# Causal attention: the exponentials of one head taken bank by bank, in three operations in place of one

## The chip, the core and the metric

One core of a Trainium2 chip runs the whole program: TensorE (PE), VectorE (DVE), ScalarE (ACT), GpSimd (POOL) and the DMA queues each work through an instruction list of their own in order and meet only at semaphores. The metric is the device time of one execution in microseconds (us).

## The reference, cut to what matters

A decoder block: causal self-attention over 4 sequences of 512 rows (16 heads of 32 columns, rotary positions), residual and layer norm, cross attention on a top-54 selection, a second norm, and a feed-forward stage with eight weighted experts. The change lies in the first part only:

```python
scale = jnp.float32(1.0 / np.sqrt(HEAD_DIM))
scores = jnp.einsum('bhqd,bhkd->bhqk', qf, kf) * scale
causal = jnp.triu(jnp.ones((S, S), dtype=bool), k=1)
scores = jnp.where(causal, -jnp.inf, scores)
weights = jax.nn.softmax(scores, axis=-1)
out = jnp.einsum('bhqk,bhkd->bhqd', weights, v)
```

## The kernel before

Stage A is the self-attention. A loop over the four sequences runs, on every engine, an order of steps written out by hand (`A_PE`, `A_ACT`, `A_DVE`, `A_POOL`), in which the heads of one sequence are interleaved with the projections of the next. A step has a name and a number: `bk.9` is step `bk` of head 9. For each head:

- `bq` (PE): scores with queries on the partitions, into banks 0 to 2. `max` (DVE, L1539) takes the negated row maxima from them, four reductions a head. Every fourth head, `mT` (PE, L987) turns four heads' maxima, and DVE (L1549) writes them as extra rows of the query operand `qcT`, so that the next scores come out with the maximum already subtracted.
- `bk` (PE, L999 and L1001): scores with keys on the partitions, into banks 3 to 5 (`st_ps`), of which there is one set. Only the causal part is computed: key block t needs 512, 384, 256 or 128 columns for t = 0 to 3. Each block is one product (L999) and one small product that adds the mask on its diagonal square (L1001). `OFF` places block 0 in bank 3, blocks 1 and 3 in bank 4, block 2 in half of bank 5: 1280 columns in a row.
- `exp` (ACT, L1253): the exponential of all 1280 columns, from the three banks into `pf[:, i % 2]`, of which there are two.
- `hi` (ACT) rounds `pf` to float16 in `phi`, and `lo` (DVE L1553 or POOL L777) writes the remainder to `plo`; 12 of the 16 heads do this (`HALVED`). Heads 3, 7, 11 and 15 don't.
- `pv` (PE): the product with the values, from `phi` and `plo` (L1018 to L1020, 30 short products) or, for those four heads, from the float32 `pf` itself (L1015, 20 products). ACT then copies the result to `osb`.

`bk` of the next head waits until `exp` of this one is through (`exp_done`), since both use the same three banks. `exp` waits for `bk` of its head (`st_ready`), and for `lo` or `pv` of two heads earlier, which free the buffer `pf`. In the program order of the last steps of a sequence, PE runs `bk.9 ... pv.7 bk.10 pv.8 ... bk.11 mT.3 pv.9 ... bk.12 pv.10 ... bk.13 pv.11 bk.14 pv.12 bk.15 pv.13`, and ACT runs `exp.9 pv.7 hi.9 exp.10 pv.8 hi.10 exp.11 pv.9 exp.12 pv.10 hi.12 exp.13 pv.11 hi.13 exp.14 pv.12`. The steps `q0`, `k0`, `q1`, `k1` (PE L962) turn the rows of Q and K for the scores; ACT copies K to `kcT` and DVE copies Q to `qcT`. The last sequence has no next one, so its engines run only the steps of its own heads, with the first weight of the cross attention (`wqw`) put in behind `pv.12` on ACT.

Stage B is the cross attention and stage C the feed-forward part; the change does not touch them. They begin when the last `pv` of stage A has been copied.

Of the kernel before, what the change touches and what calls it, by code (L numbers as in the profile page):

```python
# [16 lines left out]
ACT = mybir.ActivationFunctionType  # L17
# [7 lines left out]
H, HD, NOPE = 16, 32, 8  # L25
# [22 lines left out]
TRI = sum((i + 1) * P for i in range(TT))  # L48

OFF = {4: 0, 3: 512, 1: 896, 2: 1024}  # L50

# [214 lines left out]
def decoder(nc, a):  # L268
    ctx = ExitStack()

    def sem(name):
        return ctx.enter_context(nc.semaphore(name))
# [4 lines left out]
    with ctx:  # L277
# [139 lines left out]
        nm_ready = sem("nm_ready")  # L417
        st_ready = sem("st_ready")
        exp_done = sem("exp_done")
        p_hi = sem("p_hi")  # L420
        p_lo_pool = sem("p_lo_pool")
        p_lo_dve = sem("p_lo_dve")
# [302 lines left out]
        @block.gpsimd  # L725
        def _(pool):

            for s in [max_done, st_ready, exp_done, p_lo_pool, p_lo_dve, roped, cat_lo, nm_ready, v_moved[0], v_moved[1], comb_done, res_read,
                      att_ready, x2_kept] + \
                    [d[k] for d in (a_ready, a_drained) for k in A_PER] + [d[k] for d in (b_ready, b_drained) for k in B_BANK] + \  # L730
                    [b_low[k] for k in COPIED]:
                pool.sem_inc(s, FREE)
# [170 lines left out]
        def _(pe):  # L903
# [11 lines left out]
            def heads(seq, b, nxt, earlier, first=0, end=None):  # L915

                for n, (k, i) in enumerate(seq[:end]):
# [10 lines left out]
                    if k == "xT":  # L928

                        if i == 0:  # L930
                            pe.wait_ge(x_loaded, own * 16 + 16)
                        for t in range(TT):
                            mm = nc.tensor.transpose(bank[:, t * P:(t + 1) * P], x_in[:, t, i * P:(i + 1) * P], identf[:, :])
                        mm.then_inc(done, 1)
                    elif k == "c":

                        pe.wait_ge(w_lo, 2)
                        pe.wait_ge(a_drained["xT"], a_upto(own, ("xT", DT - 1)))
                        three(bank, lambda x, j: wkvd[:, x, j, :], lambda y, j: xT[:, y, j, :], DT, done)
                    elif k == "row":  # L940
                        ts = slice(i // 2 * P, (i // 2 + 1) * P)
                        if i == 0:
                            pe.wait_ge(w_lo, 1)
                            pe.wait_ge(a_drained["xT"], a_upto(own, ("xT", DT - 1)))
                        if i % 2 == 0:
                            three(bank, lambda x, j: xT[:, x, j, ts], lambda y, j: wq[:, y, j, :], DT, done)
                        else:
                            if i == 1:
                                pe.wait_ge(w_lo, 4)
                                pe.wait_ge(a_drained["c"], a_upto(own, ("c", 0)))  # L950
                            three(bank, lambda x, j: cT[:, x, ts], lambda y, j: wku[:, y, :], 1, done)
                    elif k == "v":
                        if i == 0:
                            pe.wait_ge(a_drained["c"], a_upto(own, ("c", 0)))
                        three(bank, lambda x, j: cT[:, x, i * P:(i + 1) * P], lambda y, j: wvu[:, y, :], 1, done)
                    elif k in ("q0", "k0", "q1", "k1"):
                        row = 2 * i + (k[0] == "k")
                        pe.wait_ge(cat_lo, own * (2 * TT) + (row + 1 + FREE))
                        out = bank.bitcast(F16)
                        for j in range(8):  # L960
                            src = cat[:, row, (k[1] == "1") * 8 + j].rearrange("p a n -> p (a n)")
                            mm = nc.tensor.transpose(out[0:K3, j * P:(j + 1) * P], src, ident16[:, :])  # L962
                        mm.then_inc(done, 1)
                    elif k in ("bq", "bqn"):

                        free = i - 1 if b is None and 0 < i < G else i
                        pe.wait_ge(max_done, (own * H + free) * 4 + FREE)
                        score = max_bank(b, i)
                        if k == "bqn" and i == 0:
                            for name in ("q0", "k0"):  # L970
                                pe.wait_ge(a_drained[name], a_upto(own, (name, TT - 1)))
                        if k == "bq" and i == 8:
                            for name in ("q1", "k1"):
                                pe.wait_ge(a_drained[name], a_upto(own, (name, TT - 1)))
                        for t in range(TT):
                            w = (t + 1) * P
                            o = OFF[t + 1]
                            nc.tensor.matmul(score[:, o:o + w], qcT[0:K3, i, t * P:(t + 1) * P], kcT[0:K3, i, 0:w],  # L978
                                             start=True, stop=False)
                            mm = nc.tensor.matmul(score[:, o + w - P:o + w], identb[:, :], mask_qk[:, :],  # L980
                                                  start=False, stop=True)
                        mm.then_inc(max_ready, 1)
                    elif k in ("mT", "mTn"):
                        pe.wait_ge(nm_ready, own * (H // G) + (i + 1 + FREE))
                        out = bank.bitcast(F16)
                        for t in range(TT):
                            mm = nc.tensor.transpose(out[:, t * P:(t + 1) * P], nm16[:, t, :], ident16[:, :])  # L987
                        mm.then_inc(done, 1)
                    elif k == "bk":

                        if i == 0:
                            pe.wait_ge(own_rows, 2)
                        if i % G == 0:
                            pe.wait_ge(a_drained["mT"], a_upto(own, ("mT", i // G)))
                        pe.wait_ge(exp_done, own * H + (i + FREE))
                        for t in range(TT):
                            w = S - t * P
                            o = OFF[TT - t]
                            nc.tensor.matmul(st_ps[:, o:o + w], kcT[0:K3 + G, i, t * P:(t + 1) * P],  # L999
                                             qcT[0:K3 + G, i, t * P:S], start=True, stop=False)  # L1000
                            mm = nc.tensor.matmul(st_ps[:, o:o + P], identb[:, :], mask_kq[:, :], start=False, stop=True)  # L1001
                        mm.then_inc(st_ready, 1)
                    elif k == "pv":

                        wait_low(pe, own, i)
                        if i not in HALVED:
                            pe.wait_ge(exp_done, own * H + (i + 1 + FREE))
                        if i % 8 == 0:
                            pe.wait_ge(v_moved[i // 8], own * 16 + (16 + FREE))
                        for q in range(TT):  # L1010
                            out = bank[:, q * (HD + 1):(q + 1) * (HD + 1)]
                            for t in range(q + 1):
                                o = OFF[TT - t] + (q - t) * P
                                if i not in HALVED:
                                    mm = nc.tensor.matmul(out, pf[:, i % 2, o:o + P], vcat[:, place(i), t, :], start=t == 0, stop=t == q)  # L1015
                                    continue
                                high, low = vcat_halved[:, place(i), t, 0:HD + 1], vcat_halved[:, place(i), t, HD + 2:2 * HD + 2]
                                nc.tensor.matmul(out, phi[:, i % 2, o:o + P], high, start=t == 0, stop=False)  # L1018
                                nc.tensor.matmul(out[:, 0:HD], phi[:, i % 2, o:o + P], low, start=False, stop=False)
                                mm = nc.tensor.matmul(out, plo[:, i % 2, o:o + P], high, start=False, stop=t == q)  # L1020
                        mm.then_inc(done, 1)
# [180 lines left out]
        def _(act):  # L1202
# [5 lines left out]
            def heads(seq, b, nxt):  # L1208
                for k, i in seq:
# [34 lines left out]
                        scaled(dst, rows[:, i % 4].unsqueeze(2).to_broadcast([P, H, 2, HD]), 1.0).then_inc(cat_hi, 1)  # L1244
                    elif k == "exp":
                        g = own * H + i
                        act.wait_ge(st_ready, g + (1 + FREE))
                        of, before = (own, i - 2) if i >= 2 else (own - 1, i + H - 2)
                        if before in HALVED:
                            wait_low(act, of, before)  # L1250
                        else:
                            act.wait_ge(a_ready["pv"], a_upto(of, ("pv", before)))
                        nc.scalar.activation(pf[:, i % 2, :], st_ps[:, 0:TRI], ACT.Exp,  # L1253
                                             scale=1.0 / (SQ * SQ * math.sqrt(HD))).then_inc(exp_done, 1)
                    elif k == "hi":
                        g = own * H + i
                        act.wait_ge(exp_done, g + (1 + FREE))
# [688 lines left out]
```

## Time and profile before

| | us |
|---|---|
| median of 3 runs | 1645.51 (1641.74 to 1646.3) |
| the profiled execution | 1652.47 |
| its span from first to last instruction | 1650.6 |
| stage A's four passes, in that span | about 98 to 457 |

The profile is of one execution. Its rows give start times in us from the start of the span, and durations. A matmul's row lasts longer than it keeps the array from the next one, since matmuls are pipelined: the distance from start to start is what a stream costs. The same holds for two ACT operations in a row. PEclk is TensorE's granted clock as a share of 2.4 GHz.

### The profile page before, as it was taken

What the parts mean: (1) busy time and instruction counts of PE and PEld (TensorE: products, weight loads), DVE (VectorE), ACT (ScalarE), POOL (GpSimd) and SP (SyncE); (2) the same over time, 40 slices, a digit from 0 to 9 for tenths busy, and PEclk for the clock granted to TensorE, in tenths of its full rate; (3) what the DMA queues carried; (4) which work ended last, traced back from release to release, by engine and by line L of the source; (5) the groups of instructions that cost most, each with busy time, mean ns of one, the idle gap of its engine ahead of it and who ended that gap; (6) DMA issues with size and microseconds to landing.
All of it is one profiled execution on the core that took longest, in us unless ns stands there. A gap on an engine that the chain in (4) does not pass through costs nothing.

```text
span 1650.6 us, 27696 instructions
## 1 busy us (share of the span) xinstructions
PE 1468.6 (89%) x10404; PEld 900.5 (55%) x10404; DVE 1193.6 (72%) x2027; ACT 900.6 (55%) x1448; POOL 777.5 (47%) x693
## 2 busy tenths in 40 slices
PE   6788887987778898577899999999999999999984
PEld 2356656565644444233555665566556655665554
DVE  2767696978359999976766676767677667767757
ACT  3447576765545544455565556555655565456542
POOL 2726171631123214678554465446644664456422
PEclk8878899997589999878999999999999999999998
DMA  9500010003010200120000100010011001000002
GB/s 287 207 26 2 28 53 29 27 15 116 27 51 27 77 29 23 51 77 14 26 27 26 39 27 26 28 38 26 27 35 30 26 26 39 26 26 27 14 1 102
DMA packets 68148, 74.68 MB, mean 45 GB/s; under 512 B 9008, under 2 KB 46512, under 8 KB 66992
## 3 DMA queue, kind: packets, MB, share of 16 engines
q1 hardware_dynamic: 67440, 68.68, 12.8%
q10 hardware_dynamic: 576, 4.19, 0.7%
q8 instruction: 88, 1.44, 0.4%
q14 instruction: 44, 0.36, 0.1%
HBM read 49.66 MB, written 10.49 MB: 36 GB/s over the span
## 4 chain that ended last, share of the span: by engine, by line
PE 66%; DVE 15%; issue 9%; ACT 4%; POOL 4%; SPq 1%; DMA 0%; DVEq 0%; ACTq 0%; POOLq 0%
PE banks L1161 48%; PE banks L908 7%; DVE nmf L1539 3%; PE banks L1015 2%; PE banks L978 2%; PE banks L962 2%; PE banks L999 2%; ACT pf L1253 1%; DVE top L1663 1%; DVE wk L1659 1%; DVE cat L1522 1%; DVE attf L1670 1%; POOL mid L885 1%; PE banks L980 1%; PE banks L1108 1%
## 5 line engine op out<-in xcount | busy, mean ns | idle before, releaser
L1161 PE MATMUL banks<-xc,w 128*128 128x512 f16 x2688 | 587.8, 381 | 16.6 <-ACT banks L1204 16.6
L1161 PEld LDWEIGHTS banks<-xc,w 128*128 128x128 f16 x2688 | 263.3, 98 | 335.3 <-ACT banks L1204 22.7
L1161 PE MATMUL banks<-wd,mid 128*128 128x256 f16 x2688 | 298.2, 273 | 5.2 <-ACT banks L1204 3.1
L1161 PEld LDWEIGHTS banks<-wd,mid 128*128 128x128 f16 x2688 | 263.5, 98 | 40.9 <-ACT banks L1204 3.4
L885 POOL TENSOR_TENSOR mid<-m,mid 128x512 f16<-128x512 f32 x64 | 74.5, 1164 | 316.2 <-ACT mid L1204 316.1
L1204 ACT ACTIVATE banks<-banks 128x512 f32<-128x512 f32 x192 | 108.4, 578 | 185.6 <-PE banks L1161 185.5
L885 POOL TENSOR_TENSOR mid<-msum,mid 128x512 f16<-128x512 f32 x128 | 185.7, 1470 | 1.3 <-ACT mid L1204 1.3
L1485 DVE SCALAR_TENSOR_TENSOR w<-stage,w 128x512 f16<-128x512 f32 (+1 forms) x56 | 61.4, 1137 | 106.1 <-ACT w L1204 106.1
L1204 ACT ACTIVATE mid<-msum 128x512 f16<-128x512 f32 x128 | 81.1, 634 | 85.5 <-DVE msum L1846 29.2
L1539 DVE TENSOR_REDUCE nmf<-banks 128x1 f32<-128x512 f32 (+3 forms) x256 | 107.3, 481 | 19.7 <-PE banks L980 19.2
L777 POOL TENSOR_TENSOR plo<-pf,phi 128x1280 f16<-128x1280 f32 x24 | 63.5, 2650 | 122.1 <-ACT phi L1204 122.0
L1253 ACT ACTIVATE pf<-banks 128x1280 f32<-128x1280 f32 x64 | 79.2, 1237 | 45.2 <-PE banks L1001 25.5
L767 POOL TENSOR_TENSOR turn_a<-rows,cossin 128x384 f32<-128x384 f32 x32 | 36.6, 1145 | 123.8 <-ACT rows L1204 122.8
L1204 ACT ACTIVATE xc<-banks 128x512 f32<-128x512 f32 (+1 forms) x112 | 62.8, 599 | 49.9 <-PE banks L1108 28.9
L885 POOL TENSOR_TENSOR mid<-xc,mid 128x512 f16<-128x512 f32 x32 | 52.5, 1641 | 69.3 <-ACT mid L1204 69.3
L999 PE MATMUL banks<-qcT,kcT 100*128 100x512 f16 (+3 forms) x256 | 70.9, 353 | 12.5 <-ACT pf L1253 11.8
L978 PE MATMUL banks<-kcT,qcT 96*128 96x128 f16 (+3 forms) x256 | 67.2, 339 | 14.8 <-DVE nmf L1539 13.6
L1485 DVE SCALAR_TENSOR_TENSOR wd<-stage,wd 128x512 f16<-128x512 f32 (+1 forms) x32 | 29.6, 966 | 65.7 <-ACT wd L1204 65.7
L1808 DVE TENSOR_TENSOR xc<-banks,xc 128x512 f32<-128x512 f32 x96 | 63.1, 681 | 17.3 <-ACT banks L1204 17.2
L1808 DVE TENSOR_TENSOR s<-banks,s 128x512 f32<-128x512 f32 x96 | 64.1, 683 | 14.2 <-PE banks L1161 14.2
L1204 ACT ACTIVATE s<-banks 128x512 f32<-128x512 f32 x96 | 56.3, 602 | 27.0 <-PE banks L1161 26.9
L1204 ACT ACTIVATE phi<-pf 128x1280 f16<-128x1280 f32 x48 | 60.9, 1270 | 0.9 <-PE banks L1020 0.9
(252 smaller groups left out, 2981.6 us busy)
## 6 DMA issues: line engine op xcount, KB each, us to landing
stage<-w_fold SPq DMA_DIRECT2D x24, 256.0 KB, 3.0
stage<-in_Wg SPq DMA_DIRECT2D x24, 256.0 KB, 3.1
stage<-in_Wu SPq DMA_DIRECT2D x24, 256.0 KB, 3.1
stage<-in_Wd SPq DMA_DIRECT2D x24, 256.0 KB, 2.8
vcat<-vnext SPq DMA_DIRECT2D x8, 528.0 KB, 3.4
x_in<-in_x SPq DMA_DIRECT2D x4, 1024.0 KB, 6.6
x_res<-in_x SPq DMA_DIRECT2D x4, 1024.0 KB, 6.0
c_raw<-in_ctx SPq DMA_DIRECT2D x4, 1024.0 KB, 5.5
```

The source lines that it names most:

```text
L767: nc.gpsimd.tensor_tensor(dst[:, :, :, :], pair, cs, ALU.mult).then_inc(roped, 1)
L777: nc.gpsimd.tensor_tensor(plo[:, i % 2, :], pf[:, i % 2, :], phi[:, i % 2, :], ALU.subtract).then_inc(p_lo_pool, 1)
L885: nc.gpsimd.tensor_tensor(mid16[:, v % 3, 1, blk], mid_value(name), mid16[:, v % 3, 0, blk], ALU.subtract)\
L908: mm = nc.tensor.matmul(out, l(x, i), r(y, i), start=(i == 0 and j == 0), stop=(i == n - 1 and j == 2))
L978: nc.tensor.matmul(score[:, o:o + w], qcT[0:K3, i, t * P:(t + 1) * P], kcT[0:K3, i, 0:w], start=True, stop=False)
L999: nc.tensor.matmul(st_ps[:, o:o + w], kcT[0:K3 + G, i, t * P:(t + 1) * P], qcT[0:K3 + G, i, t * P:S], start=True, stop=False)
L1161: mm = nc.tensor.matmul(out, l(x, i), r(y, i), start=start and i == 0 and j == 0, stop=stop and i == k - 1 and j == 2, skip_group_check=True)
L1204: return nc.scalar.activation(out, in_, ACT.Copy, scale=scale)
L1253: nc.scalar.activation(pf[:, i % 2, :], st_ps[:, 0:TRI], ACT.Exp, scale=1.0 / (SQ * SQ * math.sqrt(HD))).then_inc(exp_done, 1)
L1485: return stt(out=out, in0=src, scalar=scale, in1=hi, op0=ALU.mult, op1=ALU.subtract)
L1539: nc.vector.tensor_reduce(nmf[:, t, i % G:i % G + 1], max_bank(b, i)[:, o:o + w], AX, ALU.max, negate=True)\
L1808: tt_(saved, banks[:, k, :], saved, ALU.add).then_inc(c_sum, 1)
```

## The change

`exp` of a head becomes three ACT operations, of 512, 512 and 256 columns, one for each bank. The first two signal a new semaphore `exp_part`, the last signals `exp_done` as before. PE issues the blocks of `bk` in the order 0, 1, 3, 2, so that bank 4 is complete before bank 5 is begun; after block 0 and after block 3 it signals another new semaphore, `st_part`, and after block 2 `st_ready` as before. Before blocks 0, 1 and 2 PE waits only for the previous head's exponential of that one bank, where one wait for all three stood ahead of block 0. Each of the three ACT operations waits for the scores of its own bank.

```diff
+ST_ORDER = (0, 1, 3, 2)
+ST_FIRST = (0, 1, 2)
+ST_LAST = (0, 3, 2)
+ST_COLS = ((0, 512), (512, 1024), (1024, 1280))
...
@@ PE, bk
-                        pe.wait_ge(exp_done, own * H + (i + FREE))
-                        for t in range(TT):
+                        for t in ST_ORDER:
+                            if t in ST_FIRST:
+                                part = ST_FIRST.index(t)
+                                if part < 2:
+                                    pe.wait_ge(exp_part, (own * H + i) * 2 + (part - 1 + FREE))
+                                else:
+                                    pe.wait_ge(exp_done, own * H + (i + FREE))
...
                             mm = nc.tensor.matmul(st_ps[:, o:o + P], identb[:, :], mask_kq[:, :], start=False, stop=True)
+                            if t in ST_LAST[:2]:
+                                mm.then_inc(st_part, 1)
                         mm.then_inc(st_ready, 1)
@@ ACT, exp
-                        act.wait_ge(st_ready, g + (1 + FREE))
...
-                        nc.scalar.activation(pf[:, i % 2, :], st_ps[:, 0:TRI], ACT.Exp,
-                                             scale=1.0 / (SQ * SQ * math.sqrt(HD))).then_inc(exp_done, 1)
+                        for part, (c0, c1) in enumerate(ST_COLS):
+                            if part < 2:
+                                act.wait_ge(st_part, g * 2 + (part + 1))
+                            else:
+                                act.wait_ge(st_ready, g + (1 + FREE))
+                            nc.scalar.activation(pf[:, i % 2, c0:c1], st_ps[:, c0:c1], ACT.Exp,
+                                                 scale=1.0 / (SQ * SQ * math.sqrt(HD))).then_inc(exp_part if part < 2 else exp_done, 1)
```

## Rows read from the trace of the kernel before

**Rows 1.** Stretches: PE, PEld, DVE, ACT, POOL busy us, then PEclk, DMA, GB/s.

```profile
282.00:374.00 92.00, 80.44 (x975) 59.19 (x976) 73.61 (x133) 65.87 (x86) 43.51 (x38) 0.96 0.08 25
405.00:457.00 52.00, 39.53 (x448) 32.70 (x447) 24.71 (x35) 25.83 (x35) 10.35 (x12) 0.60 0.06 21
```

**Rows 2.** Waits in stage A, 98 to 457: total us, times, longest.

```profile
ACT pf L1253 <- PE banks L1001: 25.5, 27, 4.4
ACT pf L1253 <- PE banks L1015: 19.8, 8, 4.7
PE banks L999 <- ACT pf L1253: 11.8, 12, 1.4
```

**Rows 3.** Chain that ended last, shares by line, 98 to 457.

```profile
by line: issue 12.7%; DVE nmf L1539 10.8%; PE banks L1015 9.3%; PE banks L999 8.0%; PE banks L978 7.1%; PE banks L908 6.7%; PE banks L962 6.2%; ACT pf L1253 4.8%; PE banks L1001 3.1%; PE banks L980 2.8%; ACT kcT L1204 2.6%; DVE cat L1522 2.
```

**Rows 4.** The same chain in time, last sequence: start us, us, what.

```profile
416.29 1.25 ACT pf L1253
...
421.63 1.25 ACT pf L1253
...
428.07 1.24 DVE qcT L1549
...
434.04 4.23 PE banks L1015 x20
...
438.35 1.25 ACT pf L1253
...
442.49 0.27 ACT osb L1204
```

**Rows 5.** The same chain in the third pass, `exp.13` and `bk.14`.

```profile
358.05 1.25 ACT pf L1253
...
359.34 0.39 PE banks L999
```

**Rows 6.** ACT in order of time, third pass: start us, us, operation.

```profile
306.13 0.59 ACT L1204 ACTIVATE rows<-banks 128x512 f32<-128x512 f32 x1
306.61 1.06 ACT L1204 ACTIVATE cat<-rows 128x1024 f16<-128x1024 f32 x1
...
343.63 1.24 ACT L1253 ACTIVATE pf<-banks 128x1280 f32<-128x1280 f32 x1 [1.16 <-PE banks L1015]
344.76 0.28 ACT L1204 ACTIVATE osb<-banks 128x132 f32<-128x132 f32 x1
344.92 1.02 ACT L1204 ACTIVATE kcT<-banks 96x1024 f16<-96x1024 f16 x1
...
348.27 1.28 ACT L1204 ACTIVATE phi<-pf 128x1280 f16<-128x1280 f32 x1
349.43 1.03 ACT L1204 ACTIVATE kcT<-banks 96x1024 f16<-96x1024 f16 x1
```

**Rows 7.** PE in order of time, last sequence: `bk.9`, then `bk.10` to `bk.11`.

```profile
417.58 0.39 PE L999 MATMUL banks<-qcT,kcT 100*128 100x512 f16 x1 [0.58 <-ACT pf L1253]
...
418.38 0.22 PE L978 MATMUL banks<-kcT,qcT 96*128 96x128 f16 x1
...
422.92 0.61 PE L999 MATMUL banks<-qcT,kcT 100*128 100x512 f16 x1 [1.39 <-ACT pf L1253]
...
423.43 0.53 PE L999 MATMUL banks<-qcT,kcT 100*128 100x384 f16 x1
...
423.86 0.42 PE L999 MATMUL banks<-qcT,kcT 100*128 100x256 f16 x1
...
424.18 0.31 PE L999 MATMUL banks<-qcT,kcT 100*128 100x128 f16 x1
...
424.39 0.23 PE L1018 MATMUL banks<-vcat,phi 128*128 128x33 f16 x1
...
425.26 0.19 PE L1020 MATMUL banks<-vcat,plo 128*128 128x33 f16 x1
425.93 0.61 PE L999 MATMUL banks<-qcT,kcT 100*128 100x512 f16 x1 [0.48 <-ACT pf L1253]
```

**Rows 8.** PE in the third pass: end of `bk.2`, then `k1.2`.

```profile
295.50 0.22 PE L1001 MATMUL banks<-mask_kq,identb 128*128 128x128 bf16 x1
295.79 0.31 PE L962 MATMUL banks<-ident,cat 128*96 128x128 f16 x2
```

**Rows 9.** DVE at the same time.

```profile
294.97 0.69 DVE L1529 COPY qcT<-banks 96x1024 f16<-96x1024 f16 x1 [0.39 <-PE banks L962]
```

## What it does to the time: the prediction, before the changed kernel was run

> **What bounds the kernel now.** I read the busy times of the stretches first, then the waits of stage A, then the chain that ended last, and only then single instructions. Stage A takes some 359 us of the span. In one inner pass no engine is full: PE 80 us of 92, DVE 74, ACT 66 [rows 1]. The reader is to see that the pass hangs on the order in which the engines hand work to each other. In the last sequence's second half (405 to 457), where only its own heads are left, PE is busy 40 us of 52, DVE and ACT half the time, and TensorE's granted clock is 0.60 on average, so much of it runs at the lower level of 1.2 GHz [rows 1].
>
> The waits say how much the change can touch. ACT stands 25.5 us in all for `bk` before an exponential, and another 19.8 us for the float32 `pv` that frees its buffer; PE stands 11.8 us for exponentials before `bk` [rows 2]. Those are upper limits. The chain says how little of it counts: over stage A, L1253 holds 4.8% of the chain, some 17 us, which is about 14 of the 64 exponentials; the rest of the time DVE's reductions, the projections and the transposes are last [rows 3]. So the change is worth something only at those places, and I price them one by one.
>
> **The price of three ACT operations.** Spacing from start to start is what counts on a busy ACT: 1.13 us for the 1280 columns (343.63 to 344.76), 0.16 for 132 columns (344.76 to 344.92), 0.48 for 512 columns out of PSUM (306.13 to 306.61) [rows 6]. A line through the first two is 0.05 us fixed and 0.845 ns a column, and gives 0.48 for 512, as measured. Two more operations therefore cost 2 x 0.05 = 0.10 us a head: 0.48 + 0.48 + 0.27 = 1.23 in place of 1.13. No row shows two exponentials of one head in a row, so the bounds are 0 below and, above, no overlap at all: the durations 0.59 + 0.59 + 0.38 = 1.56 (the last on a line between 0.28 and 1.24) less 1.24, so 0.32 us. I take 0.10, since operations that wait for semaphores already satisfied stand in these same rows at the close spacing. From the start of the first part to the end of the third it is then 0.48 + 0.48 + 0.38 = 1.34 us, and the first part is done after 0.59, the second after 1.07.
>
> The Trainium skill speaks against the split here: ScalarE: Activation LUTs, section What ACT_TABLE_LOAD costs, gives an ACTIVATE with immediate scale a fixed 186 ns, of which about 93 overlap when two follow each other. By that page the split costs about 0.19 us a head (an estimate), and the sum below would be 0.5 us smaller. The trace, with 0.05 us fixed, makes it cheaper.
>
> **The price of two more waits on PE.** Where the semaphore is long satisfied I take nothing. After `bk.9`, `bq.15` has a wait in front of it and starts 418.38, 0.80 us after `bk.9` started, with no gap [rows 7]. The nearest thing that speaks against it is `k1.2`: it starts 0.29 us after the last mask product of `bk.2`, which occupies only 0.06, so 0.23 us of gap [rows 8]. But DVE's copy, which frees its bank, ends 295.66, just before [rows 9]: that gap is a wait satisfied late. Bounds: 0 and 0.23 us a wait. The new increments and the order 0, 1, 3, 2 move no column and cost nothing; they are covered by PE's own pipeline, and without that cover would cost at most what a wait does. Queued behind PE's new waits are the rest of `bk` and the next `pv` or `bq`; behind ACT's, the `osb` copy and `hi`. None of them would run earlier today, because the single wait they replace ended later or as late. The wait for the freed `pf` now stands ahead of the scores' wait, which changes nothing, since both must pass.
>
> **What a link gains at the lower clock.** `bk.10` starts 422.92, 1.29 us after `exp.9` (421.63) [rows 4, 7]. Its blocks take 0.51, 0.43, 0.32 and 0.21 us with their masks, 1.47 in all, and `pv.8` follows with 30 products up to 425.29, so 0.90 [rows 7]. I count from the start of `exp.9`. Before: `bk.10` from 1.29 to 2.76, `bk.11` from 4.30 (425.93) [rows 7]. After: block 0 can start at 0.59 + 0.05 = 0.64 (0.05 being the step from 1.24 to 1.29) and ends 1.15; blocks 1 and 3 end 1.58 and 1.79 (the second part was done at 1.07); block 2 ends 2.11 (the third was done at 1.34). `pv.8` ends at 3.01. ACT meanwhile runs `exp.9`, `osb` and `hi`: 1.23 + 0.16 + 1.16 (348.27 to 349.43 [rows 6]) = 2.55, when `exp.10` starts; its first part is done at 3.14, so `bk.11` starts at 3.19 and ends block by block at 3.70, 4.13, 4.34 and 4.66 (the third part is done at 3.89). Before, it ended at 4.30 + 1.47 = 5.77. So `bk.11`, and behind it `mT.3` and DVE's copy at 428.07 [rows 4], come 1.1 us earlier.
>
> The next links, in the same way. `bk.12` waits for DVE's copy; `exp.12` starts when bank 3 is ready instead of all three, and `bk.13` no longer waits behind the whole of it. DVE's copy, now at 5.34, is followed by `bk.12` at 6.63 (1.24 for the copy [rows 4] and the step of 0.05), blocks done 7.14, 7.57, 7.78 and 8.10; `exp.12`'s parts are done about 7.97, 8.63 and 8.90; `pv.10` ends 9.00, and `bk.13` runs right behind it, so the float32 `pv.11` starts at about 10.65 instead of 12.41 (434.04 [rows 4]): 0.65 us more. Then `exp.13`, which waits for `pv.11`, and `bk.14` are one more link; there ACT's order sets the end: `exp.13`, `osb`, `hi.13`, `exp.14`, and the copy of `pv.12` stands 2.55 + 1.23 = 3.78 us after `exp.13`, where it stands 4.14 now (438.35 to 442.49 [rows 4]): 0.35. One link earlier, `bk.9` stood 0.58 us idle for `exp.8` (416.29) at the upper clock [rows 4, 7]; `pv.6` lies between, and with it the idle goes: 0.55.
>
> Last sequence: 1.1 + 0.65 + 0.35 + 0.55 = 2.65 us. What is late next there is ACT and DVE with `wqw`, which follow `pv.12` on ACT directly and so move with it, then the last `pv`, then stage B, whose first work waits for that.
>
> **The three passes before.** Around 343 to 349 ACT runs without a pause from `exp.9` to the K copy at 349.43 [rows 6], for which PE waits; all scores are there, so two split exponentials make it 2 x 0.10 = 0.20 us later. Then `exp.13` to `bk.14` (358.05 to 359.34 [rows 5]) gains: `bk` takes 0.80 us at the upper clock [rows 7], so it ended at 1.29 + 0.80 = 2.09; after, block 2 ends at 1.34 + 0.05 + 0.17 = 1.56. That is 0.53. Net 0.33 a pass; POOL's remainder for head 13, whose `hi` comes 0.3 us later behind two split exponentials, holds it to about 0.25 at `pv.13`. Elsewhere in the pass DVE is last and exponentials have slack. Three passes: 0.75 us.
>
> **Sum.** 1652.47 - 2.65 - 0.75 = 1649.1 for the profiled execution, 3.4 us or 0.2% less. It stands 7 us above the median of the runs, so on the median's scale 1645.5 - 3.4 = 1642.1. A measurement of this kernel can tell about 0.3%, 4.9 us, from no change, so the forecast is no change that can be told. With the bounds of the ACT price (0 to 0.32 a part-split head) the sum is about 1641 to 1644.
>
> **Rivals.**
> - *The clock comes along.* In the last sequence the clock is full at `bk.9` and half from `bk.10` on, after PE stood 1.39 us [rows 7]. The change shortens that stop to about 0.64. If the upper level holds to `pv.11`, that one costs some 2.2 us less than its 4.23 [rows 4] and three groups `bk` on the chain 0.67 each (1.47 against 0.80): 4.2 us more, 1638. Against it: stops of 0.5 us remain at every head. The same thing with the other sign: the clock stays low where it is now high (`bk.9`, `bq.15`, `pv.7`), about 3.8 us, which gives 1646. The Trainium skill, TensorE: Matmul & The Clock Gate, section A second HAM failure mode, describes frequent short idles between groups of matmuls making the clock swing; that would be this second sign. No row here shows which.
> - *The gain does not arrive.* ACT's price is at its upper end and the gains of the links go to it: three passes at 2 x 0.32 - 0.53 = +0.1 each, the last sequence with four links at 0.22 less each, 1.8. Then 1644.
> - *Slower: each new wait holds back PE's next weight load.* If a wait costs the 0.23 us of [rows 8] even when satisfied, then with L999 on 8.0% of 359 us of chain [rows 3], about 29 us, at 0.56 to 1.04 us of it a group, some 40 groups are on the path: 40 x 2 x 0.23 = 18 us, 1660. It decides from (4.9 + 3.4) / 80 = 0.10 us a wait. Against it stands the late release that explains that gap.
> - *It does not do what it says:* if ACT still begins after all scores (its own order holds it), only the price is left, 1646. That lies inside the case before.
>
> **Chances.** Forecast 0.48 (its own range 1640 to 1645), clock with gain 0.24, gain lost or clock lost 0.15, slower by waits 0.13. Faster by over 0.3%: the clock case and 0.07 of the forecast's edge, 0.31. Within: 0.56. Slower: 0.13. The range takes in the clock case and the start of the slow one and leaves out about 0.2: 1636 to 1650.
>
> **What would show it.** Right: three ACT rows a head of about 0.59, 0.59 and 0.38 us, close together where scores are ready; PE's waits for ACT before `bk` shrinking by half; the copy of `pv.12` about 2.6 us nearer to `exp.8`; ACT's idle before exponentials [rows 2] smaller, most of it worth nothing. Wrong: gaps of 0.2 us inside `bk` groups whose exponential is long done; part spacing over 0.6 us; another granted clock after 415; or DVE's reductions moving, which the sum holds still.

## The result, and the profile after

The changed kernel took 0.9946 of the time of the one before, 95% interval 0.9926 to 0.9966, from 20 runs of each (medians 1643.81 and 1651.4 us). One run of the changed kernel took 2205.66 us at a granted clock of 0.64, where the others have 0.94, and is left out of the ratio. The ratio is worth 8.9 us, between 5.6 and 12.2. The forecast was 3.4 us less, too little to be told from no change. The profiled execution of the changed kernel has a span of 1642.1 us, where the one before had 1650.6.

Single executions of one kernel scatter by some 12 to 20 us: in the fourteen profiled ones the first transposes of the inner passes begin anywhere between 88.2 and 98.6 us, in code that no kernel here changes. So spans say little, and the traces are compared by stretches that begin and end at the same instruction. Landmarks are the starts of the float32 products `pv.3`, `pv.7`, `pv.11` and `pv.15` of the last sequence.

Line numbers have moved: `exp` is L1272 (before: L1253), `bk` L1012 (L999), its mask L1014 (L1001), float32 `pv` L1030 (L1015), ACT's copies L1219 (L1204), POOL's `lo` L785 (L777), DVE's normalisation L1601 (L1582).

First, stage A's waits in the changed kernel (columns as in rows 2):

```profile
ACT pf L1272 <- PE banks L1030: 16.0, 8, 3.1
PE banks L1012 <- ACT pf L1272: 5.5, 9, 1.1
ACT pf L1272 <- PE banks L1014: 4.3, 5, 1.5
```

ACT's wait for scores ahead of an exponential fell from 25.5 to 4.3 us, PE's wait for exponentials from 11.8 to 5.5 [rows 2]. Now the windows (columns as in rows 1): one inner pass, and the last 52 us before stage B starts, which in time lie 10.5 us earlier than the window of [rows 1]:

```profile
279.20:371.20 92.00, 80.78 (x966) 58.85 (x967) 73.14 (x132) 67.73 (x119) 43.38 (x38) 0.96 0.07 24
394.46:446.46 52.00, 42.18 (x502) 33.90 (x501) 31.81 (x56) 32.81 (x65) 10.70 (x12) 0.72 0.12 44
```

The pass is as before. The end of the last sequence is not: more work fits into 52 us, and TensorE's granted clock is 0.72 on average in place of 0.60 [rows 1].

Where that comes from is seen on PE, in order of time, from `pv.7` to `pv.11`:

```profile
413.64 2.37 PE L1030 MATMUL banks<-vcat,pf 128*128 128x33 f32 x20
416.70 0.39 PE L1012 MATMUL banks<-qcT,kcT 100*128 100x512 f16 x1 [0.69 <-ACT pf L1272]
...
419.28 0.61 PE L1012 MATMUL banks<-qcT,kcT 100*128 100x512 f16 x1
...
422.39 0.39 PE L1012 MATMUL banks<-qcT,kcT 100*128 100x512 f16 x1
422.67 0.33 PE L1012 MATMUL banks<-qcT,kcT 100*128 100x384 f16 x1
422.90 0.22 PE L1012 MATMUL banks<-qcT,kcT 100*128 100x128 f16 x1
423.01 0.27 PE L1012 MATMUL banks<-qcT,kcT 100*128 100x256 f16 x1
...
424.91 0.38 PE L1012 MATMUL banks<-qcT,kcT 100*128 100x512 f16 x1
...
425.71 2.37 PE L1030 MATMUL banks<-vcat,pf 128*128 128x33 f32 x20
```

`bk.10` starts after a pause of 0.69 us, where it was 1.39, and its first product takes 0.39 us, where it took 0.61 [rows 7]. `bk.11` falls to the lower level (0.61), `bk.12` and `bk.13` are at the upper one again, and so is `pv.11`: 2.37 us, 4.42 before. The granted clock of the same two stretches, `pv.7` to `pv.11` and `pv.11` itself, first in the kernel before, then after:

```profile
419.17:433.83 14.66, 11.83 (x148) 9.38 (x147) 5.72 (x10) 9.22 (x11) 5.23 (x2) 0.61 0.01 2
433.83:438.25 4.42, 4.42 (x22) 4.29 (x20) 1.33 (x1) 0.00 (x0) 0.00 (x0) 0.50 0.00 0
```

```profile
413.64:425.70 12.06, 9.90 (x148) 7.75 (x147) 6.65 (x9) 8.57 (x20) 5.20 (x2) 0.86 0.01 2
425.70:428.08 2.38, 2.38 (x22) 2.26 (x20) 1.31 (x1) 1.04 (x1) 0.00 (x0) 1.00 0.01 3
```

0.50 and 1.00 are the levels of 1.2 and 2.4 GHz. Next, ACT:

```profile
341.49 1.36 ACT L1272 ACTIVATE pf<-banks 128x512 f32<-128x512 f32 x3 [1.19 <-PE banks L1030]
342.73 0.30 ACT L1219 ACTIVATE osb<-banks 128x132 f32<-128x132 f32 x1
...
421.46 1.36 ACT L1272 ACTIVATE pf<-banks 128x512 f32<-128x512 f32 x3
...
424.05 1.36 ACT L1272 ACTIVATE pf<-banks 128x512 f32<-128x512 f32 x3 [1.05 <-POOL plo L785]
```

Three parts are shown as one row (x3) of 1.36 us where the single operation took 1.24; from the start of `exp.9` to the start of the next copy are 1.24 us where it was 1.13 [rows 6]. The last two rows are `exp.11` and `exp.12` of the last sequence. They no longer wait for scores: POOL's `lo.9` and `lo.10`, back to back from 418.81 to 424.01, hold their buffers:

```profile
418.81 5.20 POOL L785 TENSOR_TENSOR plo<-pf,phi 128x1280 f16<-128x1280 f32 x2 [12.28 <-ACT phi L1219]
```

The last rows were no part of the prediction. The first fence is the kernel before in another execution, ACT, DVE and POOL around `exp.5` of the last sequence, the second the changed kernel. The DVE row marked x4 is four operations, and the row below it is the fourth of them alone:

```profile
399.24 1.28 ACT L1253 ACT_TABLE_LOAD   x1
401.93 1.24 ACT L1253 ACTIVATE pf<-banks 128x1280 f32<-128x1280 f32 x1 [1.41 <-PE banks L1001]
...
403.24 4.21 DVE L1582 TENSOR_SCALAR resid<-resid,mv,rstd 128x512 f32<-128x512 f32 x4
404.62 2.84 DVE L1582 TENSOR_SCALAR resid<-resid,mv,rstd 128x512 f32<-128x512 f32 x1
...
404.55 2.62 POOL L777 TENSOR_TENSOR plo<-pf,phi 128x1280 f16<-128x1280 f32 x1 [19.80 <-ACT phi L1204]
```

```profile
399.88 1.28 ACT L1272 ACT_TABLE_LOAD   x1 [1.79 <-PE banks L1014]
401.18 1.36 ACT L1272 ACTIVATE pf<-banks 128x512 f32<-128x512 f32 x3
...
402.11 1.92 DVE L1601 TENSOR_SCALAR resid<-resid,mv,rstd 128x512 f32<-128x512 f32 x4
403.49 0.54 DVE L1601 TENSOR_SCALAR resid<-resid,mv,rstd 128x512 f32<-128x512 f32 x1
...
403.92 2.62 POOL L785 TENSOR_TENSOR plo<-pf,phi 128x1280 f16<-128x1280 f32 x1 [18.04 <-ACT phi L1219]
```

Before, the table load for the exponential runs ahead of the wait for scores, inside the pause; after, it follows that wait. And the four normalisations of DVE take 4.21 us before and 1.92 after. The difference lies in the fourth one: in the kernel before POOL's `lo.5` begins 0.07 us ahead of it and it lasts 2.84 us, after the change `lo.5` begins 0.43 us behind it and it lasts 0.54.

### The profile page after: what moved, and what is told of

Same layout as the page of the kernel before. It is cut to its first block, busy times and chain, and to the rows that moved or that the text cites. A ratio compares the mean times of both kernels' runs of the same rounds, so it can differ in the third digit from the quotient of the medians.

```text
span 1642.1 us, 27967 instructions
## 1 busy us (share of the span) xinstructions
PE 1466.6 (89%) x10404; PEld 897.5 (55%) x10404; DVE 1193.5 (73%) x2027; ACT 907.7 (55%) x1576; POOL 777.2 (47%) x693
## 4 chain that ended last, share of the span: by engine, by line
PE 64%; DVE 14%; issue 12%; POOL 6%; ACT 3%; SPq 1%; DMA 0%; DVEq 0%; POOLq 0%; ACTq 0%
PE banks L1176 48%; PE banks L916 7%; DVE nmf L1558 2%; PE banks L986 2%; PE banks L970 1%; PE banks L1030 1%; POOL plo L785 1%; DVE top L1682 1%; DVE wk L1678 1%; PE banks L1012 1%; DVE cat L1541 1%; DVE attf L1689 1%; PE banks L1123 1%; POOL mid L893 1%; POOL xsum L820 1%
## 5 line engine op out<-in xcount | busy, mean ns | idle before, releaser
L1219 ACT ACTIVATE banks<-banks 128x512 f32<-128x512 f32 x192 | 108.4, 578 | 185.6 <-PE banks L1176 185.5
L1504 DVE SCALAR_TENSOR_TENSOR w<-stage,w 128x512 f16<-128x512 f32 (+1 forms) x56 | 61.5, 1137 | 106.0 <-ACT w L1219 106.0
L1219 ACT ACTIVATE mid<-msum 128x512 f16<-128x512 f32 x128 | 81.1, 634 | 85.5 <-DVE msum L1865 29.2
L785 POOL TENSOR_TENSOR plo<-pf,phi 128x1280 f16<-128x1280 f32 x24 | 63.1, 2635 | 114.0 <-ACT phi L1219 114.0
L1272 ACT ACTIVATE pf<-banks 128x512 f32<-128x512 f32 (+1 forms) x192 | 87.5, 533 | 22.3 <-PE banks L1030 16.0
L1219 ACT ACTIVATE xc<-banks 128x512 f32<-128x512 f32 (+1 forms) x112 | 62.8, 598 | 49.9 <-PE banks L1123 28.9
L986 PE MATMUL banks<-kcT,qcT 96*128 96x128 f16 (+3 forms) x256 | 66.8, 338 | 12.2 <-DVE nmf L1558 11.0
L1012 PE MATMUL banks<-qcT,kcT 100*128 100x512 f16 (+3 forms) x256 | 66.5, 333 | 6.2 <-ACT pf L1272 5.5
L1219 ACT ACTIVATE s<-banks 128x512 f32<-128x512 f32 x96 | 56.2, 603 | 26.9 <-PE banks L1176 26.9
L1219 ACT ACTIVATE phi<-pf 128x1280 f16<-128x1280 f32 x48 | 61.5, 1281 | 2.1 <-PE banks L1035 2.1
```

The lines of the kernel that those rows point to most:

```text
L785: nc.gpsimd.tensor_tensor(plo[:, i % 2, :], pf[:, i % 2, :], phi[:, i % 2, :], ALU.subtract).then_inc(p_lo_pool, 1)
L1219: return nc.scalar.activation(out, in_, ACT.Copy, scale=scale)
L1272: nc.scalar.activation(pf[:, i % 2, c0:c1], st_ps[:, c0:c1], ACT.Exp, scale=1.0 / (SQ * SQ * math.sqrt(HD))).then_inc(exp_part if part < 2 ...
L1504: return stt(out=out, in0=src, scalar=scale, in1=hi, op0=ALU.mult, op1=ALU.subtract)
```

## The experiments

Theory A: the gain lies in the last sequence, where scores and exponentials alternate. Theory B: it is what the forecast's sum says, 2.65 us there and 0.25 us in each pass. Theory C, formed after the first four runs: most of the gain in the last sequence is TensorE's upper clock. (In the expectation for last_only, C still means that the gain is an accident of the clock and of the time at which DVE and POOL meet.) Ratios are to the kernel before, on the same chip, with 95% intervals. The table has the stretches of each trace, in us from start to start ("to B": from `pv.15` to ACT's first operation of stage B that writes `cxT`).

| | ratio | `pv.3` to `pv.7` | to `pv.11` | to `pv.15` | to B |
|---|---|---|---|---|---|
| before | 1 | 22.92 | 14.66 | 15.98 | 6.92 |
| before, again | | 24.52 | 14.11 | 15.97 | 6.92 |
| after | 0.9946 (0.9926 to 0.9966) | 18.69 | 12.06 | 13.57 | 6.92 |
| after, again | | 18.69 | 12.06 | 13.56 | 6.91 |
| last_only | 0.9944 (0.9920 to 0.9969) | 18.69 | 12.05 | 13.56 | 6.92 |
| inner_only | 1.0013 (0.9986 to 1.0039) | 21.77 | 14.62 | 15.99 | 6.92 |
| act_half | 0.9980 (0.9957 to 1.0002) | 20.37 | 13.64 | 15.76 | 6.92 |
| pe_half | 0.9948 (0.9920 to 0.9977) | 20.33 | 12.49 | 13.56 | 6.92 |
| price | 1.0001 (0.9971 to 1.0030) | 22.01 | 15.10 | 16.22 | 6.91 |
| fill_before | 0.9981 (0.9955 to 1.0007) | 24.53 | 12.49 | 15.00 | 6.86 |
| fill_after | 0.9959 (0.9933 to 0.9985) | 19.95 | 12.39 | 15.31 | 6.86 |
| fill_scores | 0.9983 (0.9954 to 1.0013) | 24.51 | 12.57 | 13.38 | 6.91 |
| tail_heads | 0.9934 (0.9911 to 0.9958) | 19.95 | 12.84 | 13.56 | 6.92 |
| tail_fill | 0.9929 (0.9903 to 0.9955) | 19.95 | 12.61 | 13.46 | 4.57 |

`pv.3` itself is at the upper clock in before (2.37 us), partly so in after, after again and last_only (2.8), and at the lower one (4.42) in all others. With the same exponentials that makes 1.3 to 1.6 us in the first of these stretches (18.69 against 19.95, 22.92 against 24.52). The columns are compared with this in mind.

**Where: last_only and inner_only.** The head sets say in which heads the split and the waits per bank are used.

```diff
+SPLIT_INNER = ()               # last_only; inner_only: tuple(range(H))
+SPLIT_LAST = tuple(range(H))   # last_only; inner_only: ()
...
+                        if i not in cut:
+                            act.wait_ge(st_ready, g + (1 + FREE))
+                            nc.scalar.activation(pf[:, i % 2, :], st_ps[:, 0:TRI], ACT.Exp, scale=scale).then_inc(exp_done, 1)
```

> The three-part exponential and the bank-wise waits in the last sequence only; the three passes before it as in the kernel before. Theory A (the gain comes from the last sequence, where bk and exp alternate with little else between, and the passes give about nothing): the last sequence's end comes some 8 us earlier counted from the last pass's start, as in the changed kernel, and the time is 0.994 to 0.997 of before. Theory B (the forecast's ledger, 2.65 us there and 0.25 us in each pass): 0.998. Theory C (the profile's gain in the last sequence is an accident of the clock and of the time at which DVE and POOL meet): 0.999 to 1.000.

> The reverse: the change in the three passes only, the last sequence as in the kernel before. Theory A: each pass as long as before within 0.3 us, time 0.999 to 1.001. Theory B: 0.75 us less, 0.9995. If the gain were spread over all 64 heads, three quarters of it would stand here: 0.996.

last_only gives the whole gain and inner_only none that can be told. Theory A holds, and B's 0.998 lies outside the interval of last_only. The two kernels before and after also differ in the order of ACT's two waits, and both of these have the new order in every head.

**Which wait: act_half and pe_half.** In act_half ACT takes each bank on its scores, while PE waits for the whole exponential; in pe_half PE takes the banks back one by one, while ACT waits for all scores.

```diff
@@ act_half, PE
+                        pe.wait_ge(exp_done, own * H + (i + FREE))
                         for t in ST_ORDER:
@@ pe_half, ACT
+                        act.wait_ge(st_ready, g + (1 + FREE))
                         for part, (c0, c1) in enumerate(ST_COLS):
```

> Half of the change: ACT runs the three parts, each on its bank's scores, but PE waits for the whole exponential of the previous head before bk, as before. By the prediction's rows exp.10 then starts 2.55 us after exp.9 instead of 3.01, but bk.11 only at 3.94 (before 4.30, with both halves 3.19). If both halves matter alike, half the gain is left; by these rows a third: the last sequence 1 to 3 us shorter, time 0.998 to 0.999.

> The other half: PE takes each bank as soon as its exponential is through, but ACT waits for all scores of a head before its three parts. By the prediction's rows ACT's own order (exp, osb, hi, 2.55 us) is later than the scores (2.35), so nothing is lost by that wait: the last sequence nearly as short as in the changed kernel, 6 to 8 us less than before, time 0.995 to 0.997. If starting ACT early is what pays, it is close to before.

PE's side carries most of the gain: from `pv.3` to stage B, pe_half takes 53.3 us, act_half 56.7, inner_only 59.3. In pe_half `pv.11` took 2.37 us, in act_half 4.42. That suggested theory C. Over all fourteen traces `pv.11` is at the upper clock in the seven in which PE takes the banks early, and otherwise only in fill_before and fill_scores below; it is at the lower one in before (both executions), inner_only, act_half and price.

**The clock alone: fill_before, fill_scores and fill_after.** The kernel before gets spare products on PE in the last sequence, into a bank that no one reads any more; all its waits and operations stay, and one wait is added, for the row maxima that free this bank.

```diff
+            def keep_busy(n, first=False):
+                if first:
+                    pe.wait_ge(max_done, B * H * 4 + FREE)
+                for _ in range(n):
+                    nc.tensor.matmul(banks[:, 0, 0:P], ident16[:, :], ident16[:, :], start=True, stop=True)
...
@@ ahead of bk's wait
+                        if isinstance(own, int) and own == B - 1 and i >= 10:
+                            keep_busy(6, i == 10)
@@ ahead of pv (fill_before and fill_after only)
+                        if isinstance(own, int) and own == B - 1 and i >= 14:
+                            keep_busy(24 if i == 14 else 4)
```

> The kernel before, its exponentials whole, with spare 128-column products on TensorE in the last sequence: 6 ahead of the scores of each of heads 10 to 15, 24 ahead of pv.14 and 4 ahead of pv.15 (their result is read by nothing). Theory C (what the three parts give beyond their links in the last sequence is TensorE's upper clock, which the shorter pauses between score groups keep up): with the pauses filled and nothing else changed, pv.11 and pv.15 take about 2.1 us each where they take 4.0 to 4.2, so some 2 us each and the score groups beside them a little; 3 to 5 us faster than before, ratio 0.997 to 0.998. Rival (the links do it all, the clock only goes along): pv.11 may come out at 2.1 us and the end hardly moves, 0.9995 to 1.001; and the fill itself costs where it stands on the path, up to 0.35 us for each of the 6 heads, 2 us, 1.001.

> The same spare products in the changed kernel. There pv.11 is at the upper clock already, and pv.15 alone still took 4.08 us. Theory C: pv.15 falls to about 2.1 us, so some 2 us faster than the changed kernel, 0.993 against before. Rival (links): no different from the changed kernel, 0.9945, or 1 to 2 us slower by the fill, 0.9955.

> The kernel before with only the 6 spare products ahead of the scores of heads 10 to 15 in the last sequence (none ahead of pv.14 and pv.15, where in the run with the long fill they ended 1.2 us after pv.14 could have started). Theory C (the upper clock gives most of it): from pv.7 to pv.15 some 26.3 us, where the kernel before took 30.64, the changed kernel 25.63 and the run with the long fill 27.49; pv.11 at 2.4 us from first start to last end; 4 us faster than before, 0.997 to 0.998. Rival (the waits for banks themselves give it): pv.7 to pv.15 no less than 29 us, 0.999 to 1.000.

fill_scores, PE, POOL and ACT in order of time and then the windows from `pv.7` to `pv.11` and of `pv.11` (in this kernel the fill is L918, `bk` L1007, `exp` L1261, float32 `pv` L1023; the POOL row is `lo.9` and `lo.10`, the ACT row `exp.12`):

```profile
413.27 0.50 PE L918 MATMUL banks<-ident 128*128 128x128 f16 x6
414.82 0.39 PE L1007 MATMUL banks<-qcT,kcT 100*128 100x512 f16 x1 [1.05 <-ACT pf L1261]
...
416.17 5.20 POOL L777 TENSOR_TENSOR plo<-pf,phi 128x1280 f16<-128x1280 f32 x2 [16.94 <-ACT phi L1212]
...
421.54 1.24 ACT L1261 ACTIVATE pf<-banks 128x1280 f32<-128x1280 f32 x1 [1.15 <-PE banks L1009]
...
423.63 2.37 PE L1023 MATMUL banks<-vcat,pf 128*128 128x33 f32 x20
```

```profile
411.06:423.62 12.56, 11.19 (x172) 9.26 (x171) 5.84 (x9) 8.51 (x11) 5.20 (x2) 0.86 0.01 3
423.62:426.00 2.38, 2.38 (x26) 2.38 (x24) 1.49 (x1) 0.49 (x1) 0.00 (x0) 1.00 0.00 0
```

With whole exponentials and nothing but the pauses filled, the clock is that of the changed kernel (0.86, 1.00), and `pv.7` to `pv.15` takes 25.95 us, where before took 30.64 and 30.08 and after 25.63. So 4.1 to 4.7 us come with the clock, and with the clock held the change adds 0.3. The whole time moved as expected only within its interval, which also holds no change; the stretch decides. In fill_before and fill_after the 24 products ahead of `pv.14` started late and ran at the lower clock, 2.74 us, so the stretch from `pv.11` to `pv.15` lost 1.6 us against fill_scores (15.00 against 13.38) and 1.7 against the changed kernel (15.31 against 13.57). `pv.15` stayed at 4.4 us in both, and both expectations failed there; for fill_after the rival came, some 2 us slower than the changed kernel from `pv.7` to `pv.15` (27.69 against 25.63).

**The price: price.** Both sides wait for the whole; only the three operations are left.

```diff
+                        pe.wait_ge(exp_done, own * H + (i + FREE))
...
+                        act.wait_ge(st_ready, g + (1 + FREE))
                         for part, (c0, c1) in enumerate(ST_COLS):
```

> Three operations per head, but ScalarE waits for all three banks' scores ahead of the first, and TensorE waits for the last operation ahead of the next head's scores: the price of the split with neither of its gains. By the spacing of 0.10 us more for each head (as the changed kernel's trace has it), on the path for the five or six exponentials of the last sequence and two of each pass that stand in the chain: 1 to 1.5 us slower than before, 1.0005 to 1.001. Rival (the price is larger where scores wait for the whole, since nothing then hides it): 0.3 us a head for 16 heads, 5 us, 1.003. If this kernel came out faster than before, the gain would not be that of the waits for banks at all.

1.0001 fits 0.10 us a head and does not exclude 0.3. From `pv.3` to `pv.15` price takes 0.95 us more than inner_only (53.33 against 52.38), for eleven exponentials, so 0.09 us each.

**Fewer heads, and a fill that holds: tail_heads and tail_fill.** Both split the last sequence and only heads 11 to 15 of the passes. tail_fill adds 40 spare products right behind `pv.13`.

```diff
-SPLIT_INNER = ()
+SPLIT_INNER = (11, 12, 13, 14, 15)
@@ tail_fill, behind pv's last product
+                        if isinstance(own, int) and own == B - 1 and i == 13:
+                            keep_busy(40)
```

> Split in the last sequence for all heads and in the three passes for heads 11 to 15 only, where ScalarE and TensorE alternate at the end of a pass; heads 0 to 10 of the passes keep the whole exponential. By the prediction's own steps of a pass (0.20 us lost at heads 9 and 10, 0.53 us won from head 13 to head 14): 0.2 to 0.5 us better in each pass than the kernel with the last sequence alone, so 1 us in all, 0.994. Rival (a pass's length is not set by these steps): the same as the kernel with the last sequence alone, 0.9945 within 0.001.

> The kernel split in the last sequence and in heads 11 to 15 of the passes, with 40 spare products right behind pv.13 of the last sequence, in the 3.2 us in which TensorE waits for the exponential and the lower halves of head 14. Theory C: if TensorE holds its upper clock through them, pv.15 falls from 4.1 to 2.1 us of issue, 2 us faster than the same kernel without the fill, 0.992. Rival: TensorE is at its lower clock when the fill starts (its scores ahead of pv.13 took 1.68 us where 0.95 is the upper clock's), then the 40 products take twice as long, pv.14 starts about 1 us later and pv.15 gains nothing: 0.9935 to 0.994.

tail_heads came out 0.001 better than last_only and after, far inside the intervals, so neither its theory nor its rival is shown. tail_fill, PE, the fill and `pv.15`; behind it `pv.15` in the changed kernel:

```profile
428.70 2.39 PE L931 MATMUL banks<-ident 128*128 128x128 f16 x40
433.47 2.42 PE L1046 MATMUL banks<-vcat,pf 128*128 128x33 f32 x20 [0.37 <-ACT osb L1237]
```

```profile
439.27 4.48 PE L1030 MATMUL banks<-vcat,pf 128*128 128x33 f32 x20 [0.37 <-ACT osb L1219]
```

The fill ran at the upper clock, `pv.15` took 2.42 us in place of 4.48, and the stretch to stage B 4.57 in place of 6.92. This is the fastest kernel here, 11.7 us below before; its interval overlaps that of the changed kernel.

**Chance or order of work.** Both kernels unchanged, once more.

> The changed kernel, unchanged, another execution with a profile: if the clock at pv.11 follows from the order of the work, pv.11 takes 2.4 us again, pv.7 to pv.15 25.6 us within 0.5; if it was chance, 4.4 us and 27.5 us or more.

> The kernel before, unchanged, another execution with a profile: if the clock at pv.11 follows from the order of the work, pv.11 takes 4.4 us again, pv.7 to pv.15 30.6 us within 0.5; if it was chance, 2.4 us and 28.5 us or less. Whether the fourth normalisation of the last sequence is held for 2.3 us again beside GpSimd's operation is open: in two of five executions of this order of work it was.

Every stretch behind `pv.7` came back within 0.6 us, with `pv.11` at 2.37 us after and 4.42 before. For the kernel before, `pv.7` to `pv.15` took 30.08 us, at the very edge of the 0.5 us expected. The hold of the fourth normalisation came back as well: 2.84 us in all four traces with the old order of ACT's waits (both of before, fill_before, fill_scores), 0.54 in all ten with the new order. The expectation's count, two of five, had taken inner_only, act_half and price for the old order; they have the new one.

## Why the prediction was too small

**The figure came close by luck.** The forecast of 1642.1 us lies 1.7 us from the measured median, but it starts from 1645.5, the median of 3 runs of the kernel before, where 20 runs give 1651.4. From there the same sum gives 1648.0. The gain was 8.9 us, between 5.6 and 12.2, where 3.4 were forecast. Of the prediction's own signs, PE's waits halved (11.8 to 5.5), but the copy of `pv.12` came 5.4 us nearer to `exp.8` (20.83 against 26.20) and not 2.6, and a sign of being wrong came too: another granted clock after 415.

**The price of three operations** was 0.11 us a head, 0.10 forecast (1.24 against 1.13 from start to start). The Trainium skill, ScalarE: Activation LUTs, section What ACT_TABLE_LOAD costs, would have made it about 0.19 (an estimate); the trace disagrees. The 0.5 us that the prediction takes off by that page would be 0.9 by its own count: 0.09 at four links and at two exponentials in each of three passes.

**Two more waits on PE cost nothing.** The four products of `bk.12` start 0.28, 0.23 and 0.11 us apart (422.39 to 423.01), 0.62 in all, and no gap of 0.2 us stands inside; `bk.13` takes 0.80 us up to `pv.11` (424.91 to 425.71), as `bk.9` did before [rows 7]. A gap of 0.20 us does stand inside `bk.10` (the mask product at 416.93, which occupies 0.06, and the next block at 417.19), but there the second part of `exp.9` ends only at about 417.12 (its start at 416.05 and the 1.07 of the forecast): a wait satisfied late. The slow rival falls.

**What a link gains: the step that failed.** The prediction held the clock as it was and gave 1.1 + 0.65 + 0.35 = 2.1 us to the links from `pv.7` on, and priced "the clock comes along" as a rival of 4.2 us with a chance of 0.24. The clock did not stay: from `pv.7` to `pv.15` the time fell by 4.5 to 5.0 us, of which the clock gives 4.1 to 4.7 without any split (fill_scores) and the links 0.3. The rival's own reasoning held: the stop ahead of `bk.10` fell to 0.69 us (0.64 forecast), and `pv.11` won 2.05 us (2.2 forecast). So the rival's size was right, and with the upper clock held the links are worth 0.3 and not 2.1. At the lower clock they are worth more: act_half, where `pv.11` stays at 4.42 us, takes 29.4 us from `pv.7` to `pv.15`, 1.2 less than inner_only (30.6) and 1.9 less than price (31.3). No run has both halves at the lower clock, so the 2.1 itself was not measured. Two things ate the links:

- POOL. The prediction named ACT and DVE as late next. `exp.12` now waits 1.05 us for POOL's `lo.10`. In fill_scores it starts 10.48 us after `pv.7`, after the change 10.41: with the clock held, the scores come 0.2 us after POOL is through (421.37 and 421.54 in its trace), and scores that come earlier are worth no more than that.
- The third link, priced at 0.35, was the clock's too. `exp.13` to the copy of `pv.12` took 3.79 us after (428.11 to 431.90; 3.78 forecast, 4.14 before). In fill_scores, with whole exponentials at the upper clock, it took 3.57: there the split costs 0.2.

**What had no step: `pv.3` to `pv.7`.** Only the idle of 0.55 ahead of `bk.9` was counted there. With `pv.3` at the lower clock in all of them, the stretch takes 24.5 us with the old order of ACT's waits, 21.8 to 22.0 with the new order and whole waits (inner_only, price), 20.3 to 20.4 with either half, and 19.95 with both. So the waits per bank give 1.8 to 2.1, over three times the 0.55 counted, and 2.5 to 2.7 go with the new order of two waits, which the prediction said "changes nothing, since both must pass". It moves the table load of 1.28 us behind the wait for scores; in the ten traces with the new order `exp.5` comes 7.8 to 8.8 us after `pv.3` where that is at the lower clock, in the old order 7.45. By that `lo.5` starts 0.43 us or more behind DVE's fourth normalisation and no longer ahead of it. The Trainium skill, SBUF — State Buffer, section SBUF: two separate sides, has VectorE and GpSimd share a pair of ports in some operations, and whoever starts first keeps it for its whole instruction. The trace agrees: DVE's operation ends 0.28 us after POOL's (407.45 against 407.17 in the trace of before, again). That the order of the waits causes it rests on which kernels have it. inner_only comes nearest to a test: in its last sequence exponentials and waits are whole, and only the order of ACT's two waits and the order of PE's four blocks differ from before. The order of the waits alone was not tried.

**The passes.** Forecast 0.25 us less each. In the third pass, from `exp.9` to `exp.13` the changed kernel takes 0.35 us more (14.77 against 14.42; 0.20 forecast up to the K copy) and from there to `exp.15` 0.46 less (5.50 against 5.96), where POOL's `lo.13` stops it, as forecast. Net 0.1. From the first transposes to the last `pv.15` of the three passes, the two executions of after take 271.6 and 269.9 us, those of before 271.3 and 268.9: no gain is to be seen, and a small loss can't be told from the scatter. From there to `pv.3` of the last sequence it is 28.1 and 28.0 us after, 27.3 and 30.4 before, so nothing can be told there either.

**Sum.** From `pv.3` to stage B the changed kernel takes 51.2 us, the kernel before 60.5 and 61.5: 9.2 to 10.3 less. By the steps: 2.5 to 2.7 hold, 1.8 and 0.3 links, 4.1 to 4.7 clock; the clock at `pv.3`, which differs between executions of the kernel before as well, makes the rest. So the clock is the largest of these, but not most of the whole. Stage B then takes 2 to 3 us longer (274.1 us to the first product of stage C, where before has 271.9 and 270.9), but price and act_half have the same (274.3 and 274.6), so that is scatter or an order of work that no run here isolates.

## What to carry to other kernels

A handoff cut finer pays twice where it shortens TensorE's pauses, and the larger part can be the clock: look at the granted clock of the stretch, and fill the pauses with spare products to see how much of a gain it is. Before counting a chain of shortened links, find the engine that is second to last at each of them; here POOL was 0.2 us behind. And the order of two waits ahead of an operation is an edit of its own: here it goes with the place of a table load of 1.28 us and with a shift of half a microsecond between two other engines.

## What the runs showed of the hardware, unexpected

- Six products of 128 columns ahead of each score group from `bk.10` on brought `pv.11` from 4.42 to 2.37 us (four of these groups stand ahead of it), 40 ahead of `pv.15` brought that from 4.48 to 2.42; 24 that began 1.86 and 2.11 us after PE's last work (fill_before, fill_after) ran at the lower clock, 2.74 us, and raised nothing.
- A DVE operation of 0.54 us that began 0.06 to 0.07 us behind a POOL operation of 2.62 us lasted 2.84 us, four times of four; begun 0.43 us ahead of it, 0.54.
- The table load of 1.28 us stands ahead of the wait for scores, in the pause (the four traces with the old order of the two waits), or behind it, on the path (the ten with the new order).
